# Attention scores of a graph kernel: the column term by DRAM instead of by TensorE, and one table of side stages per engine

## What is computed

```python
h = relu(layernorm(x))
for i in range(3):
    m = h @ weight[i]; aggr = A^T @ m            # per graph
    h = gru_cell(aggr, h)                        # r, z, n gates, 256 -> 768 twice
x = x + h
h = relu(layernorm(x)); Wh = h @ W.T
e = leaky_relu(s1[:, :, None] + s2[:, None, :], 0.2)   # s1 = Wh @ a1, s2 = Wh @ a2
x = x + softmax(where(adj == 0, -inf, e)) @ Wh
```

## Time and profile before

| | us |
|---|---|
| median of 3 runs | 1812.73 (1812.6 to 1813.08) |
| the profiled execution | 1811.33 |
| its span, first to last instruction | 1809.5 |
| PE busy | 1778.9 |
| DVE busy | 1420.0 |
| ACT busy | 1021.6 |
| POOL busy | 350.2 |

### The profile page before, as it was taken

One profiled execution on the slowest core, in us unless ns is written; L12 is line 12 of the kernel. 1 busy time (PEld: TensorE's weight loads), 2 busy tenths in 40 slices (PEclk: granted clock), 3 DMA queues, 4 the chain that ended last, 5 costly groups with the idle time before them and its releaser, 6 DMA issues.

```text
span 1809.5 us, 32208 instructions
## 1 busy us (share of the span) xinstructions
PE 1778.9 (98%) x10500; PEld 944.1 (52%) x10500; DVE 1420.0 (78%) x2827; ACT 1021.6 (56%) x1824; POOL 350.2 (19%) x758
## 2 busy tenths in 40 slices
PE   7999999999999999999999999999999999999995
PEld 5444555545555454555545555454554545555453
DVE  7668788787887877878787887878878777887877
ACT  5556555655555555555555556556556565556553
POOL 2022130311303122130311303113031221303100
PEclk9999999999999999999999999999999999999997
DMA  4223332423323223332332314223232332323121
GB/s 124 61 61 71 65 79 55 99 60 67 91 39 101 58 59 92 70 75 57 84 73 60 94 38 110 52 64 93 59 86 52 84 72 64 75 58 93 31 58 53
DMA packets 323712, 128.38 MB, mean 71 GB/s; under 512 B 239200, under 2 KB 323680, under 8 KB 323680
## 3 DMA queue, kind: packets, MB, share of 16 engines
q1 hardware_dynamic: 323680, 127.97, 30.0%
HBM read 52.96 MB, written 16.78 MB: 39 GB/s over the span
## 4 chain that ended last, share of the span: by engine, by line
PE 96%; DVE 1%; issue 1%; POOLq 0%; POOL 0%; ACT 0%; DVEq 0%
PE r_bank L332 28%; PE z_bank L332 27%; PE hn_bank L332 14%; PE in_bank L332 14%; PE s_bank L332 3%; PE w_bank L332 3%; PE nb_bank L346 2%; PE nb_bank L347 2%; PE t_bank L813 1%; PE t_bank L824 1%; DVE u_lo L1215 0%; DVE dot_terms L1169 0%; DVE x_out L1125 0%; DVE tail_max L1200 0%; DVE vt_lo L1114 0%
## 5 line engine op out<-in xcount | busy, mean ns | idle before, releaser
L917 ACT ACTIVATE n_out<-n_pre,bih 128x512 f32<-128x512 f32 x192 | 138.0, 719 | 239.9 <-DVE n_pre L1022 239.6
L926 ACT ACTIVATE ht_s<-ht 128x512 f16<-128x512 f32 x128 | 80.6, 630 | 265.1 <-DVE ht L1038 265.1
L332 PE MATMUL hn_bank<-ht_s,wh_hi 128*128 128x512 f16 x768 | 228.4, 379 | 1.7 <-PEq L447 1.7
L332 PE MATMUL r_bank<-ht_s,wh_hi 128*128 128x512 f16 x768 | 228.6, 379 | 0.0
L332 PE MATMUL z_bank<-ht_s,wh_hi 128*128 128x512 f16 x768 | 228.4, 379 | 0.0
L365 DVE TENSOR_TENSOR nb_lo<-nb_bank,nb_hi 128x512 f16<-128x512 f32 x192 | 131.2, 683 | 84.4 <-ACT nb_hi L361 84.3
L1017 DVE SCALAR_TENSOR_TENSOR n_pre<-tanh_r,hn_b 128x512 f32<-128x512 f32 x192 | 146.8, 764 | 61.8 <-ACT tanh_r L912 56.9
L309 POOL TENSOR_TENSOR ln_gnn<-stats_gnn 128x4 f32<-128x4 f32 x32 | 18.6, 580 | 887.8 <-DVE stats_gnn L260 887.8
L912 ACT ACTIVATE tanh_r<-r_bank,b_rz,down 128x512 f32<-128x512 f32 x192 | 147.0, 766 | 65.8 <-PE r_bank L332 65.8
L907 ACT ACTIVATE hn_b<-hn_bank,b_hn,down 128x512 f32<-128x512 f32 x192 | 147.7, 769 | 56.8 <-PE hn_bank L332 56.8
L1031 DVE SCALAR_TENSOR_TENSOR diff<-ht,n_out 128x512 f32<-128x512 f32 x192 | 132.0, 687 | 38.0 <-ACT n_out L917 37.7
(11 more groups left out here) (248 smaller groups left out, 3936.1 us busy)
## 6 DMA issues: line engine op xcount, KB each, us to landing
x_in<-in_x_dram SPq DMA_DIRECT2D x32, 512.0 KB, 4.0
x_res<-in_x_dram SPq DMA_DIRECT2D x32, 512.0 KB, 4.3
out_dram<-x_out SPq DMA_DIRECT2D x30, 512.0 KB, 5.3
adj_in<-in_adj_dram SPq DMA_DIRECT2D x32, 256.0 KB, 4.1
adj_att<-in_adj_dram SPq DMA_DIRECT2D x32, 256.0 KB, 4.5
h_s<-ht_s SPq DMA_TRANSPOSE x128, 3.0
ht_s<-h_s SPq DMA_TRANSPOSE x64, 3.2
out_dram<-x_out SPq DMA_DIRECT2D x4, 256.0 KB, 2.2
```

Source lines behind the costliest of these rows:

```text
L332: last = nc.tensor.matmul(bank_ap, w, d, start=start and i == 0, stop=stop and i == len(todo) - 1)
L917: nc.scalar.activation(n_out[c][:], n_pre[c][:], ACT.Tanh, bias=bih[:, 4 + c:5 + c]).then_inc(n_ready, 1)
L926: nc.scalar.activation(ht_s[layer % 2][a][:, c, 0, :], ht[a][:, c, :], ACT.Copy, scale=HSCALE).then_inc(ht_hi_ready, 1)
```

## The change

Three things. First, `scores` leaves PE: SP stores the group's s2 (128 partitions x 4 floats) into a DRAM buffer and loads its 512 floats back onto all 128 partitions, into `s2_row`, laid out [partition, node, graph]. Second, the sum of row and column leaves DVE: ACT computes it by four activations (Identity, with s1 as the bias), each reading every fourth float of `s2_row`. `s12` becomes `s1` and `s2`. The waits that kept `t_bank` apart for `residual` and `scores` go, and `dots` waits for `relu_att_ready`. Third, `SIDE` becomes a dictionary of five tables, one for each engine, and nearly all stages move by some steps. `LAST_SLOT_SIDE`, `TAIL` and the setup stay; the tail, with its own row transposes on PE, only gets the new names.

```diff
@@ the stages @@
+        s1 = both("s1", [P, GROUP], F32)
+        s2 = both("s2", [P, GROUP], F32)
+        s2_row = sb("s2_row", [P, P, GROUP], F32)
+        s2_dram = [nc.dram_tensor(f"s2_dram{a}", [P, GROUP], F32, kind="Internal").ap() for a in range(2)]
...
+                def store_s2(p, a):
+                    sp.wait_ge(dots_ready, per_group(p, a))
+                    sp.dma_start(s2_dram[a], s2[a][:]).then_inc(s2_stored[a], 16)
+
+                def load_s2(p, a):
+                    sp.wait_ge(s2_stored[a], per_load(p))
+                    wait_reached(sp, sum_ready, per_group(p, a) - 1)
+                    sp.dma_start(s2_row[:].rearrange("q t b -> q (t b)"),
+                                 s2_dram[a].rearrange("t b -> (t b)").unsqueeze(0).broadcast_to(
+                                     [P, T])).then_inc(s2_landed[a], 16)
...
-                    if a == 0 and c == 0:
-                        wait_reached(pe, sum_ready, per_group(p - 1, 1))
...
-                def scores(p, a):
-                    pe.wait_ge(dots_ready, per_group(p, a))
-                    if a == 1:
-                        pe.wait_ge(sum_ready, per_group(p, 0))
-                    else:
-                        pe.wait_ge(x1_ready, per_chunk(p, 1, 1))
-                    for b in range(GROUP):
-                        last = nc.tensor.transpose(t_bank[:, b * P:(b + 1) * P],
-                                                   s12[a][:, b, 1:2].broadcast_to([P, P]), ident[:])
-                    last.then_inc(s2_done, 1)
...
+                def scores(p, a):
+                    act.wait_ge(s2_landed[a], per_load(p))
+                    wait_reached(act, minus_max_ready, per_group(p, a) - 1)
+                    for b in range(GROUP):
+                        last = nc.scalar.activation(score[:, b, :], s2_row[:, :, b], ACT.Identity,
+                                                    bias=s1[a][:, b:b + 1])
+                    last.then_inc(sum_ready, 1)
...
                 def dots(p, a, half):
+                    dve.wait_ge(relu_att_ready, per_group(p, a))
...
-                    dve.wait_ge(s2_done, n)
-                    wait_reached(dve, prob_ready, n - 1)
-                    nc.vector.tensor_tensor(score[:], t_bank[:].rearrange("p (b t) -> p b t", b=GROUP),
-                                            s12[a][:, :, 0:1].broadcast_to([P, GROUP, P]),
-                                            ALU.add).then_inc(sum_ready, 1)
                     dve.wait_ge(sum_ready, n)
@@ the table before, slots 1 and 2 @@
-    (1, 0): [("update", 0, 0, 1, 0), ("split_state", 0, 1, 1, 0), ("transpose", 0, 1, 1, 0)],
-    (1, 2): [("neighbours", 0, 1, 0, 0), ("apply_att", 1, -1), ("load_gnn", 1, 1)],
-    (1, 4): [("update", 1, 0, 0, 0), ("split_state", 1, 1, 0, 0), ("transpose", 1, 1, 0, 0)],
-    (1, 5): [("neighbours", 0, 1, 1, 0)],
-    (1, 6): [("scores", 0, -1)],
-    (1, 7): [("split_att", 1, -1)],
-    (2, 0): [("update", 1, 0, 1, 0), ("split_state", 1, 1, 1, 0), ("transpose", 1, 1, 1, 0)],
-    (2, 1): [("softmax", 0, -1), ("dots", 1, 0, -1)],
-    (2, 2): [("neighbours", 1, 1, 0, 0), ("split_probs", 0, -1), ("probs_transpose", 0, -1)],
...
-    (2, 5): [("neighbours", 1, 1, 1, 0)],
...
-    (3, 1): [("gather", 0, 0, -1)],
@@ the tables after, in part @@
+    "pe": {
...
+        (1, 1): [("neighbours", 0, 1, 0, 0)],
+        (1, 6): [("neighbours", 0, 1, 1, 0)],
+        (2, 1): [("neighbours", 1, 1, 0, 0)],
+        (2, 7): [("neighbours", 1, 1, 1, 0)],
+        (3, 0): [("gather", 0, 0, -1)],
...
+        (5, 3): [("attend", 1, 1, -1), ("residual", 0, 1, 0)],
+        (5, 7): [("neighbours", 0, 0, 1, 1), ("residual", 1, 0, 0)],
+    "act": {
...
+        (0, 7): [("neighbours", 0, 1, 0, 0)],
+        (1, 0): [("split_state", 0, 1, 1, 0)],
+        (1, 2): [("apply_att", 1, -1)],
+        (1, 4): [("split_state", 1, 1, 0, 0), ("neighbours", 0, 1, 1, 0)],
+        (1, 6): [("scores", 0, -1)],
+        (1, 7): [("neighbours", 1, 1, 0, 0), ("split_att", 1, -1)],
+        (2, 0): [("split_state", 1, 1, 1, 0)],
+        (2, 1): [("softmax", 0, -1)],
+        (2, 2): [("split_probs", 0, -1)],
+        (2, 4): [("split_state", 0, 2, 0, 0)],
+        (2, 5): [("neighbours", 1, 1, 1, 0), ("gather", 0, 0, -1)],
...
+    "dve": {
...
+        (0, 6): [("neighbours", 1, 0, 1, 0), ("dots", 0, 1, -1), ("split_att", 0, -1)],
+        (0, 7): [("update", 0, 0, 1, 0), ("neighbours", 0, 1, 0, 0)],
+        (1, 0): [("split_state", 0, 1, 1, 0)],
+        (1, 2): [("dots", 1, 0, -1), ("update", 1, 0, 0, 0)],
+        (1, 4): [("split_state", 1, 1, 0, 0)],
+        (1, 5): [("neighbours", 0, 1, 1, 0)],
+        (1, 7): [("scores", 0, -1), ("update", 1, 0, 1, 0)],
+        (2, 0): [("split_att", 1, -1), ("split_state", 1, 1, 1, 0)],
+        (2, 2): [("neighbours", 1, 1, 0, 0)],
+        (2, 3): [("split_probs", 0, -1), ("update", 0, 1, 0, 0)],
...
+        (5, 2): [("residual", 0, 1, 0), ("stats_att", 0, 0), ("update", 1, 2, 0, 0)],
...
+    "sp": {
+        (0, 4): [("transpose", 0, 1, 0, 0)],
+        (1, 1): [("store_s2", 0, -1)],
+        (1, 2): [("load_gnn", 0, 1)],
+        (1, 3): [("load_s2", 0, -1)],
+        (1, 5): [("transpose", 0, 1, 1, 0)],
+        (1, 7): [("load_gnn", 1, 1)],
...
+        (2, 5): [("probs_transpose", 0, -1)],
+        (2, 6): [("store_s2", 1, -1)],
+        (2, 7): [("transpose", 0, 2, 0, 0)],
+        (3, 1): [("load_s2", 1, -1)],
+        (3, 2): [("transpose", 0, 2, 1, 0), ("transpose", 1, 2, 0, 0)],
...
```

More of the change, by code:

```diff
@@ L85 @@
[L85 to L101, removed]
@@ L102 @@
-    (1, 6): [("scores", 0, -1)],
-    (3, 6): [("scores", 1, -1)],
-    (4, 1): [("softmax", 1, -1)],
+    "pe": {
+        (0, 1): [("scores", 0, -1)],
+        (0, 2): [("neighbours", 1, 0, 0, 0)],
+        (0, 4): [("residual", 1, 1, -1), ("neighbours", 1, 0, 1, 0)],
+        (1, 1): [("neighbours", 0, 1, 0, 0)],
[3 more added lines that the diff above has]
+        (3, 0): [("gather", 0, 0, -1)],
+        (3, 2): [("neighbours", 0, 2, 0, 0)],
+        (3, 3): [("gather", 0, 1, -1), ("scores", 1, -1)],
+        (3, 5): [("neighbours", 0, 2, 1, 0), ("attend", 0, 0, -1)],
+        (4, 2): [("neighbours", 1, 2, 0, 0)],
+        (4, 4): [("attend", 0, 1, -1)],
+        (4, 5): [("neighbours", 1, 2, 1, 0)],
+        (4, 6): [("gather", 1, 0, -1)],
+        (5, 0): [("residual", 0, 0, 0)],
+        (5, 1): [("attend", 1, 0, -1), ("gather", 1, 1, -1)],
+        (5, 2): [("neighbours", 0, 0, 0, 1)],
+        (5, 3): [("attend", 1, 1, -1), ("residual", 0, 1, 0)],
+        (5, 7): [("neighbours", 0, 0, 1, 1), ("residual", 1, 0, 0)],
+    },
@@ new lines @@
+    "act": {
+        (0, 2): [("neighbours", 1, 0, 0, 0), ("split_att", 0, -1)],
+        (0, 3): [("neighbours", 1, 0, 1, 0)],
+        (0, 4): [("split_state", 0, 1, 0, 0)],
+        (0, 7): [("neighbours", 0, 1, 0, 0)],
[9 more added lines that the diff above has]
+        (2, 5): [("neighbours", 1, 1, 1, 0), ("gather", 0, 0, -1)],
+        (3, 1): [("split_state", 0, 2, 1, 0), ("gather", 0, 1, -1)],
+        (3, 2): [("neighbours", 0, 2, 0, 0)],
+        (3, 3): [("neighbours", 0, 2, 1, 0)],
+        (3, 4): [("split_state", 1, 2, 0, 0)],
+        (3, 6): [("scores", 1, -1)],
+        (3, 7): [("softmax", 1, -1), ("split_probs", 1, -1)],
+        (4, 0): [("split_state", 1, 2, 1, 0)],
+        (4, 2): [("neighbours", 1, 2, 0, 0), ("apply_gnn", 0, 1)],
+        (4, 4): [("neighbours", 1, 2, 1, 0)],
+        (4, 5): [("gather", 1, 0, -1)],
+        (5, 2): [("gather", 1, 1, -1), ("apply_gnn", 1, 1)],
+        (5, 4): [("neighbours", 0, 0, 0, 1)],
+        (5, 6): [("neighbours", 0, 0, 1, 1)],
+        (5, 7): [("apply_att", 0, 0)],
+    },
@@ new lines @@
+    "dve": {
+        (0, 0): [("residual", 1, 0, -1), ("update", 1, 2, 1, -1)],
+        (0, 1): [("neighbours", 1, 0, 0, 0)],
+        (0, 2): [("dots", 0, 0, -1), ("residual", 1, 1, -1)],
+        (0, 4): [("update", 0, 0, 0, 0), ("stats_att", 1, -1), ("split_state", 0, 1, 0, 0)],
+        (0, 6): [("neighbours", 1, 0, 1, 0), ("dots", 0, 1, -1), ("split_att", 0, -1)],
[8 more added lines that the diff above has]
+        (2, 3): [("split_probs", 0, -1), ("update", 0, 1, 0, 0)],
+        (2, 4): [("dots", 1, 1, -1), ("split_state", 0, 2, 0, 0)],
+        (2, 5): [("neighbours", 1, 1, 1, 0)],
+        (2, 6): [("update", 0, 1, 1, 0)],
+        (2, 7): [("split_state", 0, 2, 1, 0)],
+        (3, 3): [("gather", 0, 0, -1), ("neighbours", 0, 2, 0, 0)],
+        (3, 4): [("update", 1, 1, 0, 0), ("stats_gnn", 0, 1), ("neighbours", 0, 2, 1, 0), ("split_state", 1, 2, 0, 0)],
+        (3, 6): [("scores", 1, -1), ("update", 1, 1, 1, 0), ("gather", 0, 1, -1)],
+        (3, 7): [("split_probs", 1, -1)],
+        (4, 0): [("split_state", 1, 2, 1, 0), ("adjacency", 0, 1)],
+        (4, 2): [("attend", 0, 0, -1), ("stats_gnn", 1, 1), ("neighbours", 1, 2, 0, 0), ("attend", 0, 1, -1)],
+        (4, 3): [("neighbours", 1, 2, 1, 0)],
```

(28 more changed lines are left out.)

47 lines of the change are left out of this document (29 added, 18 removed).

## The result

The changed kernel takes 1796.18 us (median of 5 runs, 1795.3 to 1797.87) against 1812.62: ratio 0.9911, interval 0.9896 to 0.9925. That is 16.4 us less.

What follows compares the result with a forecast made beforehand. PE was taken as the bound, without holes in the loop. 1811.33 us - 13.2 for the transposes + 0 for everything else = 1798.1, or 1799.5 as a median; range 1796.5 to 1807, chance 0.81.

Steps and rivals of the forecast that it cites:

- main term: PE: 30 groups of four f32 score-row transposes leave, at 0.44 us each group, 13.2 us less.
- turn of 108.3 us: Sign of being right: the pair loop's turn lasts 108.3 us with PE busy all through.
- in the loop PE issues without a hole: PE in the pair loop: busy for 109.17 us of a 109.17 us turn, nothing left over between steps.
- 2 or 3 us of such holes: PE: holes below 0.2 us, unseen in the listing, could close, 2 or 3 us below the sum; chance 0.02.
- relief of DVE: DVE: the sum of row and column, 0.72 us, leaves; off the bound, worth nothing by itself.
- walk through the slots: Moved stages timed slot by slot: every input reaches PE in time, smallest margins 1.0 to 1.7 us, cost 0.
- Rival E: ACT: strided activations at 1.16 us each bring tanh_r0 1.8 us late, 27 us in all, 1826; chance 0.03.
- the 0.29 taken: ACT: each 128x128 Identity activation priced at 0.29 us from the exponential's row, 1.2 us per group.
- Rival D: SP's queue: store lands after 7.5 us, transposes take 5.5; PE loses 20 us, 1819; chance 0.05.
- my 2.2: SP's queue: the 2 KB store of s2 in 16-byte pieces taken to land in 2.2 us.
- 16-byte rule: ACT's strided reads: every f32 element pays for a new line; at factor two, 0.58 us each, time still 1799.5.

Runs made afterwards that it cites:

- experiment 2: New tables with the old score path (row transposes on PE, sum on DVE, no transfers): 1809.22 us, ratio 0.9982 against the kernel before.
- experiment 1: New score stages (store and load of s2, sum on ACT) in the kernel before's single shared order, without new tables: 1795.68 us, ratio 0.9908.
- Experiment 8: Kernel before with only the sum moved from DVE to four ACT activations reading PSUM; transposes and order kept: 1809.26 us, ratio 0.9978.
- experiment 3: Kernel before with each set of four row transposes of scores issued twice on PE: 1822.42 us, ratio 1.0055.
- experiment 7: Changed kernel with eight more Identity activations per group on ACT, into an unused tile: 1802.44 us.
- experiment 11: Changed kernel with s2_row graph by graph (store in 4-byte pieces) and the s2 load behind the state transpose in SP's queue: 1962.33 us.
- experiment 5: Changed kernel with s2_row laid out graph by graph, so activations read contiguous floats and the store writes 4-byte pieces: 1988.18 us, ratio 1.0954.
- experiment 9: Kernel before with s2 going by store and load instead of transposes, the sum left on DVE, old order: 1823.49 us, ratio 1.0059.
- experiment 12: Changed kernel with the residual's loop transposes moved from PE to DMA and DVE's slot 0 reordered, nb_lo first: 1803.31 us, ratio 0.9944.
- experiment 10: Changed kernel with the loop's remaining f32 transposes off PE: final state as f16 parts through DMA transpose, added by DVE: 1805.32 us, ratio 0.9957.

## Why the prediction was off

- **The main term holds.** 30 sets at 0.44 us: experiment 2 against the changed kernel gives 1809.22 - 1796.18 = 13.0, experiment 1 against experiment 8 gives 13.6. The turn of 108.3 us came as forecast too: 108.27.
- **The step that failed is "in the loop PE issues without a hole".** It rested on a busy time equal to the turn, a list of waits without a recurring one and the starts of a single slot. The busy time and PE's own list are blind to a wait shorter than the overlap of two products. The second stretch of rows 2 was taken for a turn and was 0.2 us short of it, and the slot was one of the first turn, which has no hole. There were 0.21 us in 13 pairs, 2.8 us in all, and the sum gave them 0. The text did allow for 2 or 3 us of such holes, but gave them a chance of 0.02 and let the range end above them. The list of waits of the weight loads, or the starts of one instruction in three pairs running, would have shown them.
- **The relief of DVE, costed at nothing, was enough to close them.** Experiment 8 shows it alone; experiments 2 and 3 show that the tables, or more work on PE ahead of the holes, do it too. In the changed kernel the relief and the tables are both there, and either would do. They can't add up, since there are only 2.8 us to be had: 3.4 for the tables and 16.9 for the stages, each by itself, are together still 16.4.
- **The walk through the slots held.** It left tanh_r0 of slot 2 1.7 us to spare. In the trace the bank was free at 717.96 and PE took it at 719.54: 1.6. It left tanh_z0 2.2; 1.9 in the trace.

```profile
717.18 0.78 ACT L989 ACTIVATE tanh_r<-r_bank,b_rz,down 128x512 f32<-128x512 f32 x1
```

```profile
719.54 0.59 PE L406 MATMUL r_bank<-ht_s,wh_hi 128*128 128x512 f16 x2
```

- **Rival E was mispriced.** The activations take 0.52 us each and about 0.41 from one to the next, 1.4 times the 0.29 taken. But 3.3 us more per group (experiment 7) cost 6.3 us in all, not 27: the sum's lateness is partly absorbed, as the state split stands behind u_hi and hn_b anyway, and these behind an nb_hi that waits 2.2 us for PE in any case (pair 6). A delay has to be followed through every queue; subtracting it from one margin is not enough.
- **Rival D's premise was real, in another kernel.** A late store did stop PE, by 192 us, but only with 4-byte pieces. At 16 bytes it lands in 1.4 us, below my 2.2. And the way was different: experiment 11 shows that the transposes crawl even when SP doesn't wait.
- **The 16-byte rule.** The Trainium skill (SBUF — State Buffer, Door 1: The DMA port swizzle) says that accesses get full bandwidth while they stay within one 16-byte line and that each that crosses to a new line pays. The traces agree: at a step of 16 bytes ACT's activation takes 522 ns instead of 399 (experiment 5, the same but for the layout), DVE's sum 1099 instead of 692 (experiment 9, against another sum). The lengths grow by a third and by six tenths, so the factor is less than two in both.

What stays open: what holds a DMA transpose behind a scattered store, and how much of experiment 12's hole is DVE's.

## What to carry to other kernels

When one engine has no idle time, measure the turn of the loop from one start of an instruction to the next, over several turns, and compare each distance within a turn with the usual one: waits shorter than the overlap of two matmuls appear in no busy share and not in PE's list of waits. The list of the weight loads points at them. What is taken off the bound is worth its issue time only as long as the next engine keeps pace. Here the sum had to leave DVE as well, and the next 26 us taken off PE were lost again, to DVE's chain in experiment 10 and to a late transpose in experiment 12. A small transfer should be judged by its pieces rather than its bytes.

## What I had not expected of the hardware

- A store of 2 KB lands in 1.4 us in pieces of 16 bytes, and in 9.1 us in pieces of 4; behind it the issue of a DMA transpose takes up to 8.7 us instead of 1.2.
- DVE's 128x512 sum takes 1099 ns with a step of 16 bytes in one input, and 683 without in the kernel before, from PSUM; another sum of that size takes 692 (experiment 9).
- A DMA transpose that lands 3.0 us after its issue elsewhere took 4.5 to 6.4 behind four other transfers (experiment 12).
- An Identity activation of 128x128 from PSUM takes 375 ns (experiment 8), 399 from contiguous SBUF.
